# A graph network's edge stage: a third buffer of gathered rows, relu ahead of the query work, node sums added two batches behind

## The chip, the cores and the metric

One Trainium2 chip, one core. The metric is device time of one execution in microseconds, lower is better. Engines are named as in the profile: PE (TensorE), DVE (VectorE), ACT (ScalarE), POOL (GpSimd), SP (SyncE, which only issues DMAs here).

## What is computed

The layer has 6250 nodes of 256 channels and 106250 directed edges sorted by destination. Cut to the part that matters here:

```python
xn = layernorm(x)
msg = relu(xn[src] + edge_attr_256)          # 106250 x 256
agg = zeros.at[dst].add(msg)                 # node sums, 6250 x 256
h = (xn + agg) @ W1 + b1 ...                 # GNN network with batch, graph and node norms
# linear attention on xn: keys and queries centred, squared, divided by their sums
k2 = l2norm_over_nodes(k*k / (sum(k*k) + 1e-7));  q2 = l2norm_over_channels(q*q / (sum(q*q) + 1e-7))
attn = v + q2 @ (k2.T @ v) / sqrt(N);  mix = attn @ W_out + b_out
x = x + gnn + mix;  x = x + top2_of_8_experts(layernorm(x))
```

Everything is float32 in the edge stage.

## The kernel before

The program runs in stages with a barrier between them: `layernorm_stage` (normalised rows go to the DRAM table `xn_rows`, and transposed tiles stay in SBUF), `edge_mix_stage` (edges and attention, the stage of the change), `gnn_mlp_stage`, `residual_stage` and `moe_stage` (the experts).

**The edge stage** walks over NB = 104 batches of 1024 edges, 8 to a partition (EK = 8). For batch b:

- SP loads 1 MB of edge attributes into `EA[b % 3]` (L566), once the matmuls of batch b-3 are done.
- POOL gathers the source rows with eight indirect DMAs of 128 rows of 1 KB each (`gather`, L187) into `GA[b % 2]`. Before a batch with even b it waits until the rows of batch b-1 have landed (`RUN = 2`), and before each batch b >= 2 until DVE has added batch b-2.
- DVE (`add`) waits for attributes, gathered rows and `win_full` of batch b-2, and then runs eight pairs: a one-hot selection tile for the next batch (L611) and the sum of rows and attributes in place (L622).
- ACT (`relu`, L720) clears the negatives of the whole batch in one instruction.
- PE (`scatter`, L792) sums the messages into a window of 128 nodes in PSUM with eight float32 matmuls against the selection tiles, each of which the profile shows as two.
- DVE (`into_tiles`, L632) adds the window to `node_sum`, in two instructions. It does that for batch b-1 right behind `add(b)`.

**Beside the edges** the same loop carries the attention, one tile of 128 nodes per batch. In the first pass (batches 1 to 51) `keys`, `key`, `squared`, `scaled`, `fourth` and `key_sums` build the key statistics. At batch 52 `finish_keys` and `key_weights` close them. In the second pass (batches 54 to 103) `query_value` (L834 and L835), `query` (L743), `query_turns` (PE transposes, L841), `query_turned` (ACT copies them from PSUM, L757), `query_fourth` (L750), `query_norm` (L762), `mixed` (L850) and `residual` (DVE, L683 to L696, then a store by SP, L581) make the attention's output.

Order is written out by hand, one instruction stream per engine. In a batch of the second pass PE runs `query_value(t)`, `query_turns(t-1)`, `scatter(b)`, `mixed(t-1)`; ACT runs `query_fourth`, `query_turned`, then `relu(b)`, `query_norm`, `query`; DVE runs `add(b)`, `into_tiles(b-1)`, `residual(t-2)`. The window sums use two PSUM banks in turn.

## Time and profile before

| | us |
|---|---|
| median of 3 runs | 2473.62 |
| lowest, highest run | 2454.32, 2487.86 |
| span of the profiled execution | 2457.6 |
| edge stage: first gather of batch 0 to the last residual instruction | 71.0 to 1347.1 |
| gathers of batches 1 to 103 | 84.2 to 1322.3 |

The span runs from the first to the last instruction of the profiled execution. The three runs lie between 3.3 us below and 30.3 us above it, the median 16.0 us above. In the rows, a name such as `edge_attr` stands for all buffers of that name; "idle before" is how long the engine had done nothing before the instruction, and what ended that.

### The profile page before, as it was taken

How to read it: one execution, taken by the hardware profiler on the slowest of the kernel's cores; microseconds unless marked ns; L12 is line 12 of the kernel's file. 1: busy time of each engine (PE TensorE's matmuls, PEld its weight loads, DVE VectorE, ACT ScalarE, POOL GpSimd, SP SyncE). 2: the span in 40 equal slices, each digit the busy share in tenths (PEclk: the TensorE clock that was granted, in tenths of full speed). 3: DMA queues.
4: the chain of work that ended last, by engine and by line, in shares of the span. 5: the costliest groups of instructions: out<-in, count | busy, mean ns of one | idle time of the engine just before them, and what ended most of it. 6: DMA issues, size and time to landing. Idle time of an engine off the chain costs nothing. (4 is left out here: it accounts for less than half of the span.)

```text
span 2457.6 us, 34821 instructions
## 1 busy us (share of the span) xinstructions
PE 1823.5 (74%) x10022; PEld 1451.8 (59%) x10023; DVE 1286.6 (52%) x3862; ACT 823.3 (34%) x1606; POOL 1250.4 (51%) x1137
## 2 busy tenths in 40 slices
PE   3367665676667777777686889681279999999996
PEld 3245444455444555454454778571268888888885
DVE  7455455545555555554554444568954444444443
ACT  3122222222222222222222346557324444444442
POOL 1576676776776666666663000136424444444443
PEclk8587788777878877888788999755689999999998
DMA  6565565555655555655553100377213223223222
GB/s 234 175 210 186 183 200 181 195 188 184 203 182 183 189 187 191 197 184 178 183 189 123 23 1 0 94 213 222 77 25 50 43 45 48 45 44 49 45 43 35
DMA packets 129882, 320.95 MB, mean 131 GB/s; under 512 B 32234, under 2 KB 78729, under 8 KB 114427
## 3 DMA queue, kind: packets, MB, share of 16 engines
q0 software_dynamic: 66624, 157.12, 24.7%
q1 hardware_dynamic: 56908, 162.65, 19.1%
q10 hardware_dynamic: 6255, 0.10, 0.3%
q8 instruction: 36, 0.59, 0.1%
q14 instruction: 59, 0.48, 0.1%
HBM read 279.67 MB, written 40.12 MB: 130 GB/s over the span
## 5 line engine op out<-in xcount | busy, mean ns | idle before, releaser
L187 POOL DMA_INDIRECT gathered<-xn_rows,src_table x832 | 846.2, 1017 | 409.3 <-issue 253.8
L792 PE MATMUL bank<-edge_attr,dst_select 128*128 128x256 f32 x1664 | 562.9, 512 | 379.7 <-issue 194.7
L792 PEld LDWEIGHTS bank<-edge_attr,dst_select 128*128 128x128 f32 x1664 | 433.1, 267 | 506.8 <-issue 214.7
L611 DVE TENSOR_SCALAR dst_select<-iota_window,dst_partition 128x128 f32<-128x128 f32 x832 | 258.8, 312 | 379.5 <-DMA gathered<-xn_rows,src_table 315.5
L1751 PE MATMUL bank<-rowsT_parts,expert_weights 128*128 128x256 f16 x3564 | 409.5, 274 | 10.0 <-issue 6.3
L1751 PEld LDWEIGHTS bank<-rowsT_parts,expert_weights 128*128 x3564 | 346.7, 98 | 59.0 <-issue 17.9
L720 ACT ACTIVATE edge_attr<-edge_attr 128x2048 f32<-128x2048 f32 x104 | 198.3, 1906 | 514.0 <-DVE edge_attr L622 438.5
L622 DVE TENSOR_TENSOR edge_attr<-gathered,edge_attr 128x256 f32<-128x256 f32 x832 | 344.2, 414 | 0.0
L1712 POOL DMA_INDIRECT out<-expert_out,output_row_of_slot x108 | 184.2, 1705 | 300.4 <-ACTq L1810 278.0
L1857 DVE SCALAR_TENSOR_TENSOR gated<-bank,silu 128x512 f32<-128x512 f32 x216 | 120.7, 559 | 184.5 <-ACT silu L1796 172.8
L1764 PE MATMUL bank<-expert_weights,gated_parts 128*128 x1836 | 209.3, 273 | 0.4 <-DVE gated_parts L1865 0.4
L1764 PEld LDWEIGHTS bank<-expert_weights,gated_parts 128*128 128x128 f16 x1836 | 179.5, 98 | 21.5 <-issue 0.7
L1865 DVE TENSOR_TENSOR gated_parts<-gated,gated_parts 128x512 f16<-128x512 f32 x216 | 122.8, 568 | 124.9 <-ACT gated_parts L1800 124.1
L757 ACT ACTIVATE query_squaredT<-bank 128x256 f32<-128x256 f32 (+1 forms) x49 | 18.8, 383 | 452.1 <-PE bank L841 349.2
L1796 ACT ACTIVATE silu<-bank 128x512 f32<-128x512 f32 x216 | 104.6, 484 | 190.7 <-PE bank L1751 181.2
L1800 ACT ACTIVATE gated_parts<-gated 128x512 f16<-128x512 f32 x216 | 112.8, 522 | 150.0 <-DVE gated L1857 149.4
L632 DVE SCALAR_TENSOR_TENSOR node_sum<-bank,in_first_tile,node_sum 128x256 f32 x104 | 49.7, 478 | 212.7 <-PE bank L792 163.9
L67 POOL DMA_DIRECT2D out<-residual_in x20 | 14.1, 712 | 240.4 <-DVE residual_in L1369 239.9
L1702 POOL DMA_INDIRECT rows<-token_rows,row_of_slot x110 | 109.6, 997 | 50.0 <-issue 32.5
L1065 PE MATMUL bank<-activated,w_gnn 128*128 128x250 f32 x400 | 87.7, 383 | 9.0 <-ACT activated L1096 9.0
L834 PE MATMUL bank<-w_q_and_v_out,xnT 128*128 128x512 f32 (+1 forms) x196 | 92.1, 592 | 0.0
L1050 PE MATMUL bank<-node_sumT,w_gnn 128*128 128x256 f32 (+1 forms) x400 | 89.3, 377 | 0.0
(274 smaller groups left out, 2095.3 us busy)
## 6 DMA issues: line engine op xcount, KB each, us to landing
edge_attr<-in_edge_attr SPq DMA_DIRECT2D x104, 1024.0 KB
raw_weights<-in_L_ffn_w SPq DMA_DIRECT2D x16, 1088.0 KB, 5.1
gathered<-xn_rows,src_table POOLq DMA_INDIRECT x832
rows_in<-xn_rows SPq DMA_DIRECT2D x48, 128.0 KB
rows_in<-in_x SPq DMA_DIRECT2D x48, 128.0 KB
residual_rows<-residual_tile SPq DMA_DIRECT2D x48, 128.0 KB
residual_in<-residual_rows SPq DMA_DIRECT2D x10, 560.0 KB
out<-residual_in POOLq DMA_DIRECT2D x10, 560.0 KB, 4.4
```

Of the source, the lines that this page charges most:

```text
L187: pool.indirect_dma_start(out=k.GA[h][:, e, :], out_offset=None, in_=k.xn_d[:, :], in_offset=bass.IndirectOffsetOnAxis(ap=k.src[:, b, e:e ...
L611: dve.tensor_scalar(SEL[b % 3][:, e, :], k.iota[:, :], k.dstp[:, b, e:e + 1], None, ALU.is_equal)
L622: last = dve.tensor_tensor(ea[:, e, :], ga[:, e, :], ea[:, e, :], ALU.add)
L720: act.activation(EA[b % 3][:, :, :], EA[b % 3][:, :, :], ACT.Relu).then_inc(relu_done, 1)
L792: last = pe.matmul(WINP[b % 2][:, 0:C], SEL[b % 3][:, e, :], EA[b % 3][:, e, :], start=e == 0, stop=e == EK - 1)
L1702: pool.indirect_dma_start(out=XG[i % 2][:, t, :], out_offset=None, in_=k.tok_d[:, :], in_offset=bass.IndirectOffsetOnAxis(ap=k.row_of[:, a ...
L1712: pool.indirect_dma_start(out=k.acc_d[:, :], out_offset=bass.IndirectOffsetOnAxis(ap=k.sum_of[:, at:at + 1], axis=0), in_=YS[i % 2][:, t, ...
L1751: last = pe.matmul(bank[:, jj * TT:(jj + 1) * TT], w(e, wp, at + b * step, 128), X16[h][:, xp, b, :], start=n == 0, stop=n == 3 * CB - 1)
L1764: last = pe.matmul(YP[h][:, t * C:(t + 1) * C], G16[h][:, gp, j * TT + t * 128:j * TT + (t + 1) * 128], w(e, wp, W2S + j * C, C), start=n ...
L1800: last = act.activation(G16[h][at, 0, s * 512 + cols.start:s * 512 + cols.stop], GF[r][at, cols], ACT.Copy)
L1857: last = dve.scalar_tensor_tensor(GF[r][at, cols], (H1 if tail else H3)[r][at, cols], SG / (SX * SW), SIL[r][at, cols], ALU.mult, ALU.mult)
L1865: last = dve.tensor_tensor(low, GF[r][at, cols], G16[h][at, 0, to], ALU.subtract)
```

## The change

In the edge stage:

- A third buffer `gathered2` with its own semaphore (AHEAD = 3). POOL no longer waits for landed rows; before batch b it waits only until DVE has added batch b-3.
- `into_tiles` runs two batches behind `add` (LATER = 2), and `scatter(b)` gets a wait: `into_tiles(b-2)` must have emptied the PSUM bank that it writes. Until now that followed from DVE's order.
- ACT runs `relu(b)` ahead of `query_fourth` and `query_turned` of its batch.
- To make room, the query's squares and fourth powers use the key's buffers (`Q2, Q4 = K2[0:2], K2[2]`), the transposed squares use `K4`, and the residual tiles use `KB`. The first pass is done with them when the second begins.

```diff
--- before.py
+++ after.py
@@ -57,6 +57,7 @@
 
 
 
+AHEAD = 3
 SPLIT = TR // 16 * 16
 MOVED = 32
 
@@ -181,11 +182,11 @@
     return min(NP, N - t * NP)
 
 
-def gather(k, pool, b, h):
+def gather(k, pool, b, rows, done):
 
     for e in range(EK):
-        pool.indirect_dma_start(out=k.GA[h][:, e, :], out_offset=None, in_=k.xn_d[:, :],
-                                in_offset=bass.IndirectOffsetOnAxis(ap=k.src[:, b, e:e + 1], axis=0)).then_inc(k.g_in[h], 16)
+        pool.indirect_dma_start(out=rows[:, e, :], out_offset=None, in_=k.xn_d[:, :],
+                                in_offset=bass.IndirectOffsetOnAxis(ap=k.src[:, b, e:e + 1], axis=0)).then_inc(done, 16)
 
 
 def layernorm_stage(k, st):
@@ -328,7 +329,7 @@
                 store(n)
             pool.wait_ge(src_ready, 2)
             pool.wait_ge(xn_st, 16 * (NG + 1))
-            gather(k, pool, 0, 0)
+            gather(k, pool, 0, k.GA[0], k.g_in[0])
 
         @block.vector
         def _(dve):
@@ -500,8 +501,10 @@
 
     nc, sb, sem, A = k.nc, k.sb, k.sem, k.A
     two, three = range(2), range(3)
+    LATER = 2
     EA = [sb(f"edge_attr{h}", [128, EK, C], F32, st) for h in three]
-    GA, g_in = k.GA, k.g_in
+    GA = [*k.GA, sb("gathered2", [128, EK, C], F32, st)]
+    g_in = [*k.g_in, sem("gathered_in2")]
     SEL = [sb(f"dst_select{h}", [128, EK, NP], F32, st) for h in three]
     XT = [sb(f"rows_in{h}", [128, C], F32, st) for h in two]
     KB = [sb(f"key{h}", [128, C], F32, st) for h in two]
@@ -510,14 +513,13 @@
     KT = sb("key_sum_shifted", [128, 1], F32, st)
     VS = [sb(f"row_scaled{h}", [128, C + 1], F32, st) for h in two]
     K4 = [sb(f"key_fourth{h}", [128, C], F32, st) for h in two]
-    Q2 = [sb(f"query_squared{h}", [128, C], F32, st) for h in two]
-    Q4 = sb("query_fourth", [128, C], F32, st)
-    Q2T = [sb(f"query_squaredT{h}", [128, CB, NP], F32, st) for h in two]
+    Q2, Q4 = K2[0:2], K2[2]
+    Q2T = [K4[h][:, :].rearrange("p (b n) -> p b n", b=CB) for h in two]
     QS = sb("query_sums", [128, PT], F32, st)
     QF = sb("query_fourth_sums", [128, PT], F32, st)
     QN = sb("query_norms", [128, PT], F32, st)
     QD = [sb(f"query_scale{h}", [128, 1], F32, st) for h in two]
-    RT = [sb(f"residual_tile{h}", [128, C], F32, st) for h in two]
+    RT = KB
     KX = sb("key_by_node", [128, CB, C + 1], F32, st)
     KXT = sb("key_by_nodeT", [128, CB, C], F32, st)
     nrow = sb("key_norm_row", [1, C], F32, st)
@@ -539,7 +541,6 @@
         "query_value_full", "query_squared_done", "query_fourth_done", "query_norm_done", "queryT_full", "queryT_done",
         "mix_full", "residual_done"))
     stray_full, stray_out = sem("strays_summed"), sem("strays_copied")
-    RUN = 2
     P1, P2 = 1, PT + 5
     FIN = PT + 3
 
@@ -599,11 +600,9 @@
         @block.gpsimd
         def _(pool):
             for b in range(1, NB):
-                if b % RUN == 0:
-                    pool.wait_ge(g_in[(b - 1) % 2], 16 * EK * ((b - 1) // 2 + 1))
-                if b >= 2:
-                    pool.wait_ge(added, b - 1)
-                gather(k, pool, b, b % 2)
+                if b >= AHEAD:
+                    pool.wait_ge(added, b - AHEAD + 1)
+                gather(k, pool, b, GA[b % AHEAD], g_in[b % AHEAD])
 
         @block.vector
         def _(dve):
@@ -611,9 +610,9 @@
                 dve.tensor_scalar(SEL[b % 3][:, e, :], k.iota[:, :], k.dstp[:, b, e:e + 1], None, ALU.is_equal)
 
             def add(b):
-                ea, ga = EA[b % 3], GA[b % 2]
+                ea, ga = EA[b % 3], GA[b % AHEAD]
                 dve.wait_ge(ea_in[b % 3], 16 * (b // 3 + 1))
-                dve.wait_ge(g_in[b % 2], 16 * EK * (b // 2 + 1))
+                dve.wait_ge(g_in[b % AHEAD], 16 * EK * (b // AHEAD + 1))
                 if b > 1:
                     dve.wait_ge(win_full, b - 1)
                 for e in range(EK):
@@ -699,8 +698,8 @@
                 select(0, e)
             for b in range(NB):
                 add(b)
-                if b > 0:
-                    into_tiles(b - 1)
+                if b >= LATER:
+                    into_tiles(b - LATER)
                 if is_tile(b - P2 - 2):
                     residual(b - P2 - 2)
                 if is_tile(b - P1):
@@ -709,7 +708,8 @@
                     scaled(b - P1 - 1)
                 if b == FIN:
                     finish_keys()
-            into_tiles(NB - 1)
+            for b in range(NB - LATER, NB):
+                into_tiles(b)
             for t in range(NB - P2 - 2, PT):
                 residual(t)
 
@@ -762,11 +762,10 @@
                 act.activation(QN[0:v, t:t + 1], QF[0:v, t:t + 1], ACT.Sqrt).then_inc(qn_done, 1)
 
             for b in range(NB):
+                relu(b)
                 if is_tile(b - P2 - 1):
                     query_fourth(b - P2 - 1)
                     query_turned(b - P2 - 1)
-                relu(b)
-                if is_tile(b - P2 - 1):
                     query_norm(b - P2 - 1)
                 if is_tile(b - P2):
                     query(b - P2)
@@ -787,6 +786,8 @@
             pe.matmul(STRAY[0:1, 0:1], k.stray_col[:, :], k.ones[:, 0:1], start=True, stop=True).then_inc(stray_full, 1)
 
             def scatter(b):
+                if b >= LATER:
+                    pe.wait_ge(evac, b - LATER + 1)
                 pe.wait_ge(relu_done, b + 1)
                 for e in range(EK):
                     last = pe.matmul(WINP[b % 2][:, 0:C], SEL[b % 3][:, e, :], EA[b % 3][:, e, :], start=e == 0, stop=e == EK - 1)
```

## Rows read from the trace of the kernel before

**Rows 1.** The page, part 1: busy us, share of the span, instructions.
```profile
PE 1823.5 (74%) x10022; PEld 1451.8 (59%) x10023; DVE 1286.6 (52%) x3862; ACT 823.3 (34%) x1606; POOL 1250.4 (51%) x1137
```

**Rows 2.** Waits of POOL, 71 to 1340 us: engine, line, releaser, total us, times, longest.
```profile
POOL gathered L187 <- issue: 253.8, 772, 4.0
POOL gathered L187 <- DMA gathered<-xn_rows,src_table: 114.3, 49, 5.0
POOL gathered L187 <- DVE edge_attr L622: 33.6, 9, 6.1
```

**Rows 3.** Timeline of POOL, first pass, two batches: start us, duration us, instruction, idle before.
```profile
119.85 0.94 POOL L187 DMA_INDIRECT gathered<-xn_rows,src_table  x1 [2.02 <-DMA gathered<-xn_rows,src_table]
121.10 1.09 POOL L187 DMA_INDIRECT gathered<-xn_rows,src_table  x1 [0.30 <-issue]
122.50 1.29 POOL L187 DMA_INDIRECT gathered<-xn_rows,src_table  x1 [0.30 <-issue]
...
135.35 1.27 POOL L187 DMA_INDIRECT gathered<-xn_rows,src_table  x1 [0.30 <-issue]
136.94 1.29 POOL L187 DMA_INDIRECT gathered<-xn_rows,src_table  x1 [0.30 <-issue]
...
142.74 0.95 POOL L187 DMA_INDIRECT gathered<-xn_rows,src_table  x1 [2.01 <-DMA gathered<-xn_rows,src_table]
```

**Rows 4.** Timeline of DVE, first pass: the first of 16 instructions of an add, and what follows.
```profile
426.68 0.29 DVE L611 TENSOR_SCALAR dst_select<-iota_window,dst_partition 128x128 f32<-128x128 f32 x1 [6.56 <-DMA gathered<-xn_rows,src_table]
...
430.95 0.47 DVE L632 SCALAR_TENSOR_TENSOR node_sum<-bank,in_first_tile,node_sum 128x256 f32 x1
```

**Rows 5.** Busy time of every engine in the two passes.
```profile
core 0: us, PE busy (x) PEld busy (x) DVE busy (x) ACT busy (x) POOL busy (x), PEclk, DMA share, GB/s
84.00:720.00 636.00, 407.38 (x1368) 307.04 (x1369) 327.49 (x1191) 142.69 (x202) 445.06 (x435) 0.78 0.58 192
720.00:1323.00 603.00, 450.11 (x1336) 295.35 (x1335) 309.69 (x1106) 150.95 (x334) 393.42 (x390) 0.81 0.58 189
```

**Rows 6.** Waits of four engines in the second pass, 720 to 1323 us.
```profile
POOL gathered L187 <- DMA gathered<-xn_rows,src_table: 57.0, 22, 5.0
POOL gathered L187 <- DVE edge_attr L622: 33.2, 8, 6.1
...
PE bank L792 <- ACT edge_attr L720: 108.2, 29, 9.9
PE bank L792 <- issue: 44.7, 19, 3.7
...
ACT query_squaredT L757 <- remote: 102.8, 8, 14.7
...
DVE node_sum L632 <- PE bank L792: 147.9, 32, 12.9
```

**Rows 7.** Timeline of PE and ACT, one batch of the second pass.
```profile
869.48 1.03 PE L850 MATMUL bank<-kv_out_weights,query_squaredT 128*128 128x256 f32 x4
...
873.21 0.44 PE L841 MATMUL bank<-ident,query_squared 128*128 128x128 f32 x2
...
874.11 0.39 ACT L757 ACTIVATE query_squaredT<-bank 128x256 f32<-128x256 f32 x1 [9.93 <-PE bank L841]
874.39 1.90 ACT L720 ACTIVATE edge_attr<-edge_attr 128x2048 f32<-128x2048 f32 x1
...
876.34 6.68 PE L792 MATMUL bank<-edge_attr,dst_select 128*128 128x256 f32 x16 [2.70 <-ACT edge_attr L720]
...
882.86 1.03 PE L850 MATMUL bank<-kv_out_weights,query_squaredT 128*128 128x256 f32 x4
```

**Rows 8.** Timeline at the end of the stage.
```profile
1321.37 0.94 POOL L187 DMA_INDIRECT gathered<-xn_rows,src_table  x1 [0.30 <-issue]
...
1327.15 2.76 DVE L622 TENSOR_TENSOR edge_attr<-gathered,edge_attr 128x256 f32<-128x256 f32 x8
...
1346.71 0.42 DVE L696 TENSOR_TENSOR residual_tile<-residual_tile,bank 106x256 f32<-106x256 f32 x1
```

## The prediction

> **What bounds the kernel now.** I read the page first, then POOL's waits, then POOL's and DVE's timelines, and last the two passes apart. Part 1 of the page [rows 1] points at PE, busy for 74% of the span. That is an average over stages. In the edge stage the engine to look at is POOL, the one that gathers. Its waits [rows 2] are of three kinds: 253.8 us of "issue" in 772 pieces, which is 0.30 us between any two gathers with a few longer ones; 114.3 us in 49 waits for landed rows; 33.6 us in 9 waits for DVE's adds. The timeline [rows 3] shows the pattern of the first pass: 16 gathers in a row, 0.94 to 1.29 us each with 0.30 us between them, then one wait of 2.0 us until the last rows are in. A pair of batches takes 142.74 - 119.85 = 22.9 us. DVE starts its adds when the rows land, after 6.56 us of idleness, and needs 430.95 - 426.68 = 4.3 us for them [rows 4]. So in the first pass DVE, ACT and PE all hang on POOL, and POOL stops for nothing but the landing.
>
> The second pass is slower. From 84 to 720 us POOL issues 435 gathers, that is 54.4 batches at 11.7 us; from 720 to 1323 us it is 390 gathers, 48.75 batches at 12.4 us [rows 5]. POOL waits 57.0 us for rows and 33.2 us for adds there, DVE waits 147.9 us for the window sums, and PE waits 152.9 us for its messages [rows 6]. The timeline [rows 7] shows a circle: PE's transposes (873.21), ACT's copy of them (874.11), only then relu (874.39), then the scatter (876.34), which ends near 882.86 and lets DVE add the window, finish the residual and begin the next adds. Relu stands behind the copy on ACT, so 2.70 us of PE's time go by in each batch.
>
> **The change part by part.**
>
> *POOL's waits.* Both kinds are gone as long as DVE's add of batch b-3 is done when POOL begins batch b. Rows of batch b-1 land about 2 us into POOL's work on batch b, and their add takes 4.3 us; two batches earlier, the add of batch b-3 ended some 15 us before POOL wants its buffer for batch b. That is 114.3 + 33.6 = 147.9 us less [rows 2]. Each of the 58 waits leaves the ordinary 0.30 us of issue in its place, 17.4 us. Net: 130.5 us.
>
> *Gathers beside DVE.* A gather takes 0.95 us alone and up to 1.29 us beside the adds and selections. In a batch that began with a wait, POOL starts with DVE and two gathers are stretched, by 0.14 and 0.34 us (the rows at 121.10 and 122.50 in [rows 3]). In a batch without the wait they are stretched by 0.32 and 0.34 us (135.35 and 136.94 in [rows 3]). All batches will now be of the second kind: 0.2 us for each of 49, 10 us given back. Bounds: if no gather were stretched, the 824 gathers would shrink from 838.5/825 = 1.016 us [rows 5] to 0.95 us, 55 us less; if eight of eight took 1.29 us, the rival below. I take +10 us, as the unwaited batches show it.
>
> The Trainium skill speaks against this part. "SBUF — State Buffer", in "A bandwidth-pool intuition that's wrong (but worth ruling out)", says that GpSimd and a two-port DVE operation do not run together, "one fully blocks". By that rule each batch would cost eight gathers at 1.25 us plus the whole 4.3 us of adds, 14.3 us, and POOL could not go below that. The trace has batches of 10.5 us with the adds beside them, so the block holds here for part of the gathers only.
>
> *Landing of rows.* The rows must keep up with a POOL that never pauses. In the pair of [rows 3] the DMA engines followed 16 gathers and were 1.7 us behind the last (2.01 less 0.30). The longest such wait is 5.0 us [rows 2]. The DMA share is 0.58 [rows 5]; at 10.8 instead of 12.0 us a batch it becomes 0.65. I price this at nothing: a third buffer lets rows be late by most of a batch. If that cover is gone, it is the third rival.
>
> *Relu first.* ACT starts relu when the adds are done. In the second pass PE's 152.9 us of waiting [rows 6] lose their cause; PE then needs 603 - 152.9 = 450.1 us for 48.75 batches, 9.2 us each. Eight waits of ACT are marked "remote" and sum to 102.8 us, 12.9 us each against the usual 9.9 us [rows 6, 7]. I read the excess, 24 us, as something that held PE up unseen, 0.5 us a batch. So PE needs 9.7 us and POOL (603 - 90.2 + 9.0) / 48.75 + 0.1 = 10.8 us. POOL bounds this pass too, by 1.1 us. What moves behind relu (fourth powers, copy, norm) is needed by `mixed`, behind a scatter of 6.5 us; relu is 1.90 us and the copy 0.39 us [rows 7], so it is hidden.
>
> *Node sums two behind, and the new wait.* DVE no longer waits at `into_tiles`, since that window was summed a batch ago. But `residual` behind it still needs `mixed` of the batch before, which stands behind the same scatter, so in the second pass the 147.9 us of waiting mostly move to the residual's last instructions. That costs nothing while DVE has slack: it is busy 309.7 of 603 us [rows 5], 6.4 us a batch. The new wait of `scatter(b)` has `mixed` and all later PE work queued behind it, and DVE's next residual waits for those. It is met 1.0 us after the adds (two window adds of 0.47 us, the first in [rows 4]), while relu takes 1.90 us from the same point. It costs nothing; at worst, with DVE held in the residual of the batch before, the second rival.
>
> *Shared buffers.* The key tiles are last used at batch 51, the query tiles begin at 54. Nothing.
>
> *The end of the stage.* The last gather ends at 1322.3 us, the last residual at 1347.1 us [rows 8], 24.8 us later. In between the last adds begin only at 1327.15, because DVE was late with the residual. Without lag: 1.7 us landing, 2.8 us adds, 2.0 us relu, 6.5 us scatter and 1.0 us mixed [rows 7], and an estimated 2.5 us for the window's two adds and the five short instructions of the residual, 16.5 us. I take 8 us less; it could be 0, with PE still behind.
>
> *Sum.* -130.5 + 10 - 8 = -128.5 us. I add 6 us for moments in the second pass in which PE, 1.1 us a batch ahead on average, is late for longer than the buffers cover (bounds 0 and 81 us, the whole of POOL's gain there; nearest to zero, since 1.1 us a batch make up a loss quickly). That gives -122.5 us, a span of 2335.1 us. The page gives no time of the profiled execution itself; the median of the runs lies 16.0 us above its span, and with that I forecast 2351 us, 5% less. Runs of this kernel spread by 1.4%, so about 2% can be told from no change.
>
> **The rivals.**
>
> *PE becomes the bound of the second pass.* For it: PE is the busiest engine there, 450 of 603 us, and its scatter took 6.5 us of wall time in [rows 7] (876.34 to 882.86), its other work 4.2 us (869.48 to the end at 873.65), and the stalls add 0.5 us: 11.2 us a batch. With 0.3 us lost at each hand-over it is 11.5 us, 34 us more than POOL's 10.8 over the pass: 2379 us (2351 - 6 + 34). Against it: the granted clock averages 0.81 there [rows 5], and the scatters that took 6.5 us began after PE had stood idle; with less idleness it should not fall.
>
> *The rows, not POOL, set the pace (the change doesn't do what it says).* The software queue would be as fast as the pattern of 22.9 us a pair and no faster, DVE would wait as before, and only the end of the stage is saved: 2466 us. For it: waits of up to 5.0 us for landing [rows 2]. Against it: 16 gathers issued in 20.9 us were followed to within 1.7 us. "DMA: Bandwidth & Descriptors", in "Queues, rings and completion order" of the Trainium skill, says that each DMA engine takes turns between queues, a packet at a time, so a gather beside the 1 MB load of attributes gets only part of the engines. That would stretch the landing for the length of the load, not for good.
>
> *Slower.* POOL runs beside DVE's adds and beside unlanded rows all the time, and every gather takes the 1.29 us that is now the exception: 8 x (1.29 + 0.30) = 12.7 us a batch against 1238.1/103 = 12.0 us, 0.7 x 103 = 72 us more, less the end's 8 us: 2538 us. It decides from a mean gather of 1.20 us on. For it: 1.29 us is what a gather beside DVE costs. Against it: DVE's adds fill 4.3 of 10.8 us, and twelve of the sixteen gathers of [rows 3] did not exceed 0.95 us.
>
> **How the numbers follow.** Chances: forecast 0.70 (own range 2320 to 2375), PE bound 0.16 (2365 to 2400), rows set the pace wholly or in part 0.09 (2400 to 2470), slower 0.05. Predicted: 2351 us. Low end: shorter gathers could give up to 55 us, of which I allow 35: 2315 us. The high end takes in PE's case and the first part of the third: 2425 us. Faster by over 2% means below 2424 us: 0.70 + 0.16 + 0.02 = 0.88. Within 2%: 0.08. Slower: 0.04.
>
> **What would show it.** Right: POOL's waits for rows gone, gathers back to back at 0.30 us for whole passes, 10.7 to 10.9 us a batch in both, mean gather 1.02 to 1.05 us, last gather at about 1208 us, relu directly behind the adds in the second pass. PE's case: POOL waits for DVE's adds in the second pass, with PE's waits near nothing. The rows' case: DVE waits more than 6 us for rows and POOL for DVE. Slower: mean gather above 1.2 us. I am wrong at large if the stage still takes over 1200 us.

## The result, and the profile after

| | before, us | after, us |
|---|---|---|
| median of 5 runs each, in turn on one chip | 2477.99 | 2514.68 |
| lowest, highest run | 2454.32, 2487.86 | 2507.52, 2528.43 |
| span of the profiled execution | 2457.6 | 2526.8 |
| last gather issued, last residual instruction | 1322.3, 1347.1 | 1395.1, 1416.5 |

The ratio is 1.0165, with a 95% interval from 1.0115 to 1.0215: slower by 1 to 2%, where 5% faster was forecast. The whole loss lies in the edge stage, which ends 69.4 us later.

First POOL, since the forecast is a sum over POOL. These are its waits and the longest of ACT's and DVE's, from 71 to 1420 us (engine, line, releaser, total us, times, longest); they answer to [rows 2] and [rows 6]. Most lines of the changed kernel have moved by one: the gather is L188, relu L720, the adds L621, the scatter L793, `key` L639, the copies of the turned tiles L757 and the residual L693.

```profile
POOL gathered L188 <- issue: 248.8, 807, 2.1
ACT key_fourth L757 <- remote: 231.0, 13, 30.1
POOL gathered L188 <- DVE edge_attr L621: 225.8, 23, 15.0
...
ACT key_squared L727 <- DVE key L639: 202.0, 16, 23.8
DVE key L639 <- remote: 195.4, 14, 26.8
DVE key L693 <- remote: 182.1, 23, 16.7
...
PE bank L851 <- issue: 152.1, 9, 22.4
```

The waits for landed rows are gone, as the forecast said (114.3 us in [rows 2]). But 23 waits for DVE's adds stand there, 9.8 us each, where there were 9 of 3.7 us. POOL was to be free of those too. DVE in turn waits for something the profile calls "remote", up to 26.8 us at a time, and PE shows "issue" waits of up to 22.4 us. The two passes, with the columns of [rows 5]:

```profile
84.00:720.00 636.00, 382.24 (x1268) 267.00 (x1269) 301.56 (x1103) 139.56 (x196) 416.85 (x407) 0.73 0.54 179
720.00:1390.00 670.00, 412.58 (x1410) 266.20 (x1408) 322.31 (x1169) 152.82 (x327) 417.26 (x414) 0.80 0.56 180
```

In the same 636 us POOL issues 407 gathers where it issued 435, and every engine did less. No engine is the bound on average. So the place to look is what happens ahead of one of the 23 waits. This is the timeline of the changed kernel from 462 to 477 us, as PE, POOL, DVE and ACT lines stand in it (start, duration, instruction, idle before):

```profile
462.54 0.58 PE L793 MATMUL bank<-edge_attr,dst_select 128*128 128x256 f32 x1 [1.32 <-issue]
...
463.96 0.58 PE L793 MATMUL bank<-edge_attr,dst_select 128*128 128x256 f32 x1 [0.84 <-issue]
...
465.39 0.59 PE L793 MATMUL bank<-edge_attr,dst_select 128*128 128x256 f32 x1 [0.85 <-issue]
...
466.09 0.29 PEld L793 LDWEIGHTS bank<-edge_attr,dst_select 128*128 128x128 f32 x1 [1.11 <-issue]
466.79 0.59 PE L793 MATMUL bank<-edge_attr,dst_select 128*128 128x256 f32 x1 [0.81 <-issue]
...
472.14 0.94 POOL L188 DMA_INDIRECT gathered<-xn_rows,src_table  x1 [0.30 <-issue]
...
475.92 1.29 PE L799 MATMUL bank<-w_k,xnT 128*128 128x256 f32 x2 [0.81 <-issue]
...
476.71 0.42 DVE L639 TENSOR_TENSOR key<-bank,b_k_rows 128x256 f32<-128x256 f32 x1 [20.10 <-remote]
...
477.16 0.42 ACT L727 ACTIVATE key_squared<-key 128x256 f32<-128x256 f32 x1 [19.40 <-DVE key L639]
```

Look at PE's rhythm. The profile shows nothing that it waits for, yet it starts one matmul every 1.40 us, with the weight load half way between: 0.70 us for each instruction, whatever that is. A scatter of 32 instructions takes 22 us at this pace; it takes 3.6 to 6.8 us otherwise. I call such a standstill behind PE a crawl. DVE and ACT stand idle for 20 us, since all they have left depends on PE. POOL alone goes on, in steps of 1.25 us, until at 473.1 it has filled all three buffers and must stop. 2.8 us after its stop PE issues two matmuls back to back again, and POOL goes on at 482.4, when DVE has added. The stretches of this crawl one by one, with the columns of [rows 5]:

```profile
460.00:465.00 5.00, 2.38 (x5) 1.15 (x4) 0.00 (x0) 0.00 (x0) 3.78 (x5) 0.50 0.36 105
465.00:470.00 5.00, 2.16 (x4) 0.86 (x3) 0.00 (x0) 0.00 (x0) 3.78 (x5) 0.50 0.37 105
470.00:475.00 5.00, 1.83 (x4) 0.86 (x3) 0.00 (x0) 0.00 (x0) 2.48 (x3) 0.50 0.37 105
```

DMA share 0.37 at 105 GB/s: neither the engines of the DMA nor the memory are at a limit (0.54 over the pass). The granted clock is 0.50, its lower level of 1.2 GHz, but that makes a matmul 0.58 us long; it does not put 0.8 us of nothing behind it.

The rhythm is one of two faces. In the second pass most standstills look like this:

```profile
1012.46 0.44 PE L842 MATMUL bank<-ident,key_squared 128*128 128x128 f32 x2
1012.73 3.62 PE L793 MATMUL bank<-edge_attr,dst_select 128*128 128x256 f32 x16
...
1021.75 0.95 POOL L188 DMA_INDIRECT gathered<-xn_rows,src_table  x1 [0.30 <-issue]
1022.16 0.48 DVE L693 SCALAR_TENSOR_TENSOR key<-bank,query_scale,rows_in 128x256 f32<-128x256 f32 x1 [12.19 <-remote]
...
1023.00 0.95 POOL L188 DMA_INDIRECT gathered<-xn_rows,src_table  x1 [0.30 <-issue]
...
1041.08 0.38 ACT L757 ACTIVATE key_fourth<-bank 128x256 f32<-128x256 f32 x1 [30.09 <-remote]
```

By their rows PE's two transposes (L842) are done at 1012.9 and the scatter behind them at 1016.35, at full pace. ACT's copy of the transposes waits for their semaphore, and it starts at 1041.08, 28.2 us after they ended. The wait is called "remote" because no row of the program ends near the semaphore's update. So here PE's work, as recorded, is done and only its signal is late. (The ends of PE's rows are modelled, so they can be off by some part of a matmul; no model of a 0.3 us matmul makes 28 us.)

POOL pauses for over 1 us 25 times in the stage, and there are 31 stretches of over 7 us, 421 us together, in which neither DVE nor ACT does anything; before had none inside the stage. Ten of the 31 hold the rhythm of 0.70 us, nine of them in the first pass; most of the others end with a signal of PE that came over 5 us late. In 14 of them POOL's pause begins first and DVE or ACT come back 2.4 to 5.4 us later (158.1 and 163.5, 232.9 and 238.0, 346.6 and 350.8, and so on). In a fifteenth the pause begins 0.3 us before the end, and 16 end while POOL goes on issuing, as at 1022.16 above. So a stop of POOL may end a crawl, but a crawl also ends without one. Before, POOL stopped by itself every two batches.

### The profile page after: what moved, and what is told of

The parts are those of the page before. It is cut to its first block and busy times, and to the rows that moved or that the text cites. A ratio compares the mean times of both kernels' runs of the same rounds, so it can differ in the third digit from the quotient of the medians.

```text
span 2526.8 us, 34872 instructions
## 1 busy us (share of the span) xinstructions
PE 1767.0 (70%) x10022; PEld 1386.4 (55%) x10023; DVE 1280.8 (51%) x3862; ACT 825.7 (33%) x1606; POOL 1250.2 (49%) x1137
## 5 line engine op out<-in xcount | busy, mean ns | idle before, releaser
L188 POOL DMA_INDIRECT gathered<-xn_rows,src_table x832 | 845.9, 1017 | 482.3 <-issue 248.8
L793 PE MATMUL bank<-edge_attr,dst_select 128*128 128x256 f32 x1664 | 455.3, 426 | 215.1 <-issue 125.2
L793 PEld LDWEIGHTS bank<-edge_attr,dst_select 128*128 128x128 f32 x1664 | 347.4, 214 | 312.3 <-issue 225.2
L1752 PEld LDWEIGHTS bank<-rowsT_parts,expert_weights 128*128 x3564 | 346.1, 98 | 59.1 <-issue 18.2
L621 DVE TENSOR_TENSOR edge_attr<-gathered,edge_attr 128x256 f32<-128x256 f32 x832 | 344.4, 415 | 2.3 <-issue 2.3
L720 ACT ACTIVATE edge_attr<-edge_attr 128x2048 f32<-128x2048 f32 x104 | 198.6, 1910 | 384.9 <-DVE edge_attr L621 218.5
L851 PE MATMUL bank<-kv_out_weights,key_fourth 128*128 128x256 f32 (+1 forms) x196 | 63.4, 454 | 207.7 <-issue 152.1
L1765 PEld LDWEIGHTS bank<-expert_weights,gated_parts 128*128 128x128 f16 x1836 | 179.5, 98 | 21.5 <-issue 0.7
L851 PEld LDWEIGHTS bank<-kv_out_weights,key_fourth 128*128 128x128 f32 (+1 forms) x196 | 42.4, 224 | 220.4 <-issue 156.2
L639 DVE TENSOR_TENSOR key<-bank,b_k_rows 128x256 f32<-128x256 f32 (+1 forms) x49 | 20.4, 417 | 276.6 <-remote 195.4
L757 ACT ACTIVATE key_fourth<-bank 128x256 f32<-128x256 f32 (+1 forms) x49 | 18.6, 380 | 379.0 <-remote 231.0
L693 DVE SCALAR_TENSOR_TENSOR key<-bank,query_scale,rows_in 128x256 f32<-128x256 f32 (+1 forms) x49 | 23.7, 483 | 198.1 <-remote 182.1
```

Of the source, the lines that this page charges most:

```text
L188: pool.indirect_dma_start(out=rows[:, e, :], out_offset=None, in_=k.xn_d[:, :], in_offset=bass.IndirectOffsetOnAxis(ap=k.src[:, b, e:e + 1 ...
L621: last = dve.tensor_tensor(ea[:, e, :], ga[:, e, :], ea[:, e, :], ALU.add)
L720: act.activation(EA[b % 3][:, :, :], EA[b % 3][:, :, :], ACT.Relu).then_inc(relu_done, 1)
L793: last = pe.matmul(WINP[b % 2][:, 0:C], SEL[b % 3][:, e, :], EA[b % 3][:, e, :], start=e == 0, stop=e == EK - 1)
L1752: last = pe.matmul(bank[:, jj * TT:(jj + 1) * TT], w(e, wp, at + b * step, 128), X16[h][:, xp, b, :], start=n == 0, stop=n == 3 * CB - 1)
L1765: last = pe.matmul(YP[h][:, t * C:(t + 1) * C], G16[h][:, gp, j * TT + t * 128:j * TT + (t + 1) * 128], w(e, wp, W2S + j * C, C), start=n ...
```

## The experiments

The kernels ran in five sittings, each on one chip with its own runs of before; ratios are to those. The sittings differ in a way that turned out to matter, so each is given with what before took in it. "Idle stretches" are those of over 7 us with neither DVE nor ACT busy, inside the edge stage. Where POOL pauses on purpose, some of them are DVE's ordinary wait for rows and no crawl (5 in the first run below, the longest of 8.9 us).

### First sitting (before 2449.96 us): does the pause protect PE?

Theory A: POOL's unbroken stream of gathers makes PE crawl, and a pause ends or prevents it. Rivals: the new order (relu first, node sums two behind), or the third buffer itself.

The wait for landed rows put back into the changed kernel:

```diff
             for b in range(1, NB):
+                if b % 2 == 0:
+                    pool.wait_ge(g_in[(b - 1) % AHEAD], 16 * EK * ((b - 1) // AHEAD + 1))
                 if b >= AHEAD:
```

> The changed kernel with one thing undone: POOL again waits before every even batch until the rows of the batch before have landed. The third buffer, relu first, sums two behind and the shared homes stay. Theory A (an unbroken stream of gathers keeps PE from getting on; a pause of POOL ends it): PE's long crawls of 12 to 22 us are gone, POOL waits some 50 times about 2 us for rows and hardly for DVE, the stage has 10.8 to 11.7 us a batch, and the time is 2400 to 2470 us, below the kernel before. Theory B (the new order of ACT and DVE with PE's new wait makes the stalls): the crawls stay, and the time is 2500 us or more.

Measured: 2409.95 us, ratio 0.9826 (0.9796 to 0.9855), 105 us less than the changed kernel in its own sitting. POOL's waits:

```profile
POOL gathered L188 <- issue: 238.2, 779, 0.5
POOL gathered L188 <- DMA gathered<-xn_rows,src_table: 118.9, 51, 4.1
```

There is no wait for DVE left, although three buffers and the order are those of after. Adding waits of 118.9 us removed waits of 225.8 us.

The mirror image, before without its wait (two buffers, old order):

```diff
-                if b % RUN == 0:
-                    pool.wait_ge(g_in[(b - 1) % 2], 16 * EK * ((b - 1) // 2 + 1))
                 if b >= 2:
```

> The kernel before with one thing taken away: POOL's wait for landed rows before even batches. Two buffers, the old order of relu and sums and the old homes stay. Theory A: PE crawls appear here too, of 10 to 20 us about once in five batches, and the time is 2490 to 2600 us, slower than before. Theory B: no crawls, POOL's 114 us of waiting for rows turn into waiting for DVE's adds or into gain, and the time is 2380 to 2480 us.

Measured: 2537.0 us, ratio 1.0367 (1.0304 to 1.043), 14 idle stretches of 176 us, 228.5 us in 39 waits of POOL for DVE. This and the kernel before, in one sitting, differ in nothing but that wait: taking it out is enough to lose more than the whole change loses.

The third buffer with the order of before:

```diff
-    LATER = 2
+    LATER = 1
...
-                relu(b)
                 if is_tile(b - P2 - 1):
...
                     query_turned(b - P2 - 1)
+                relu(b)
+                if is_tile(b - P2 - 1):
...
-                if b >= LATER:
-                    pe.wait_ge(evac, b - LATER + 1)
```

> The changed kernel with the old order: relu behind the query work, sums one batch behind, no new wait of PE. The third buffer, no wait for landed rows and the shared homes stay. Theory A: crawls as in the changed kernel, since POOL is as free as there; 2500 to 2560 us. Theory B: crawls gone, the first pass at 10.7 us a batch, 2370 to 2430 us.

Measured: 2548.55 us, ratio 1.0387 (1.0344 to 1.0431), 16 idle stretches of 228 us. POOL's waits:

```profile
POOL gathered L188 <- issue: 251.6, 791, 2.1
...
POOL gathered L188 <- DVE edge_attr L621: 230.6, 38, 19.2
```

So the new order is not what slows the change. It may soften it: the changed kernel had 1.0165 and, below, 1.0196, in other sittings.

A pause that waits for nothing: eight small memsets, each with a drain, ahead of every even batch, in the changed kernel. Whatever has landed or not, POOL issues no gather for a while.

```diff
             for b in range(1, NB):
+                if b % 2 == 0:
+                    for _ in range(PAUSES):
+                        pool.memset(pause[:, :], 0.0)
+                        pool.drain()
```

> The changed kernel, where POOL before every even batch does eight small memsets with a drain behind each, some 2 to 4 us, and waits for no rows. Theory A, in the form that any pause in the issue of gathers is enough: crawls gone or cut to the few us until the next pause, 2400 to 2480 us. If instead it is the wait for landing that matters and not the pause: crawls stay, 2500 us or more plus some of the memsets' time. Theory B: 2500 us or more.

Measured: 2591.53 us, ratio 1.0562 (1.0529 to 1.0595). The crawls are gone, as theory A has it, and the time is far above its range, since the pause came out at 6.1 us from one gather to the next and not at 2 to 4. No wait is called "remote" (the first run has 11 such waits, 32.8 us), POOL never waits for DVE or for rows, and a pair of batches takes 26.9 us, the pause and 16 gathers of 1.01 us with 0.30 us between them. POOL's groups (busy, mean ns, idle before):

```profile
L189 POOL DMA_INDIRECT gathered<-xn_rows,src_table x832 | 840.4, 1010 | 283.6 <-issue 276.0 <-DMA xn_rows<-node_sum 4.3 <-POOLq L240 3.4
...
L607 POOL MEMSET pause_tile<- 128x128 f32 x408 | 97.7, 239 | 176.5 <-issue 142.2
```

A wait for a semaphore of the rows is not needed, then, to keep PE going. The run can't tell a pause in issuing from the landing of the rows, though: waits for rows last 2.3 us on average in the run with the landed wait (118.9 us in 51), so in 6.1 us the rows have landed too. To tell the two apart takes a shorter pause in a sitting with crawls, and no run has that.

### Second sitting (before 2430.37 us): more instructions for PE, other pauses

In the first pass of after the idle stretches begin 212 or 318 rows of PE apart (weight loads and matmuls), but for two that are 53 apart. The profile shows 16 KB packets of instructions in a DMA queue of their own:

```profile
q8 instruction: 37, 0.61, 0.1%
```

The 22 of them from 143.8 to 1405.8 us stand 255 instructions of PE apart on average ((5840 - 477) / 21, by the count of PE's records). The Trainium skill, "Runtime: NRT & Kernel Launch", "Instruction fetch mechanics", says that an engine's program arrives in blocks of 16 KiB, 256 instructions, and that the crossing is "mostly hidden". The size agrees with these packets. Once a block is about as often as the crawls come. The loads themselves are not slow, 0.9 to 1.5 us each, and they don't stand where the crawls do: 6 of the 31 idle stretches have one in them, 0.7 to 2.2 us after their start, and none ends with one. That a crawl follows from such a block is the idea that I tested: with more instructions in the program there should be more crawls. Forty waits that are always met went ahead of each scatter:

```diff
                 pe.wait_ge(relu_done, b + 1)
+                for _ in range(40):
+                    pe.wait_ge(stray_full, 1)
```

> The changed kernel with 40 more PE instructions a batch, each a wait for a semaphore that came long ago, ahead of the scatter. Theory A1 (what the stream of gathers holds up is the loading of PE's instructions, which comes once per block of its program, so that a crawl belongs to every so many instructions): the crawls come about twice as often in batches, every two to three batches instead of every five; the time rises by 150 us or more, to over 2650 us. Theory A2 (the gathers hold up PE's work itself, whatever its instructions): crawls as often as in the changed kernel; some 2 us of waits a batch lie mostly beside other work, 2500 to 2600 us.

Measured: 2319.86 us, ratio 0.9546 (0.9527 to 0.9565). No crawl at all, no idle stretch, no pause of POOL, where both theories had over 2500 us. It runs as the forecast had it. Its POOL waits and passes:

```profile
POOL gathered L188 <- issue: 252.9, 830, 0.3
```

```profile
84.00:720.00 636.00, 445.32 (x1496) 332.51 (x1497) 354.34 (x1288) 156.78 (x233) 491.96 (x473) 0.81 0.64 210
720.00:1180.00 460.00, 382.03 (x1207) 251.05 (x1206) 276.09 (x989) 130.99 (x301) 355.18 (x345) 0.86 0.69 222
```

473 gathers in 636 us are 59.1 batches at 10.76 us, and 345 in 460 us are 10.67 us a batch. A DMA share of 0.64 to 0.69 goes with no crawl here, where the crawls had 0.37: a busy set of DMA engines is not by itself what PE suffers from.

This looked as if more instructions cured PE. That was wrong, as the fourth sitting showed, and in this sitting nothing else was run that could have told it: the changed kernel itself was missing. The other three kernels were variants of the pause.

The landed wait of the first sitting ahead of every fourth batch:

```diff
+                if b % 4 == 0:
+                    pool.wait_ge(g_in[(b - 1) % AHEAD], 16 * EK * ((b - 1) // AHEAD + 1))
```

> As e1, but POOL waits for landed rows only before every fourth batch. Theory A: a pause every 46 us or so leaves room for crawls of up to two or three batches' gathers, so they come back in part: between e1 and the changed kernel, 2420 to 2500 us. If a pause every four batches is as good as one every two, the waits saved (25 times 1.7 us) show as gain: 2370 us on the scale of e1's 2410.

Measured: 2366.08 us, 0.9732 (0.9715 to 0.9748).

Ahead of every batch:

```diff
+                pool.wait_ge(g_in[(b - 1) % AHEAD], 16 * EK * ((b - 1) // AHEAD + 1))
```

> As e1, but POOL waits for landed rows before every batch. Theory A: the rest of the PE stalls (46 us in six stretches over 7 us in which DVE and ACT both do nothing, in e1) goes, but 51 more waits of 1.7 us cost 87 us of POOL's time: 2440 to 2500 us. If stalls still cost e1 much more than seen, it is below 2410 us.

Measured: 2476.54 us, 1.0193 (1.0176 to 1.021); 102 waits of 2.08 us, 211.8 us.

Three small memsets ahead of every even batch, a pause of 1.3 us on average from one gather to the next, with no regard to landing:

```diff
+                if b % 2 == 0:
+                    for i in range(PAUSES):
+                        pool.memset(pause[:, :], 0.0).then_inc(paused, 1)
+                        pool.wait_ge(paused, (b // 2 - 1) * PAUSES + i + 1)
```

> The changed kernel, where POOL before every even batch does three small memsets, each waited for by POOL itself, about 1 us, and waits for no rows. It is shorter than the 1.7 us that the last rows need to land. If any gap in the issue of gathers lets PE on: crawls gone and about 30 us less than e1, near 2380 us. If the rows in flight must have landed first: crawls stay, 2500 us or more.

Measured: 2369.99 us, 0.9752 (0.9735 to 0.9768).

None of the four crawled. So they price pauses, and say nothing on what cures PE.

### Third sitting (before 2429.96 us): what of PE's extra work matters?

Two more wide matmuls a batch instead of the waits (their result is overwritten by the scatter's first matmul):

```diff
+                for _ in range(2):
+                    pe.matmul(WINP[b % 2][:, 0:2 * C], SEL[b % 3][:, 0, :], EA[b % 3][:, 0:2, :].rearrange("p e c -> p (e c)"), start=True, stop=True)
```

> The changed kernel with two more matmuls of 512 columns a batch ahead of the scatter (their sums are overwritten by it): about 2 us more of PE's time a batch, as the 40 waits of e5 take, with 8 instead of 40 more instructions. If e5 lost its crawls because PE comes later (its pace): crawls gone here too, 2320 to 2350 us. If it is the number or the kind of instructions: crawls stay, 2500 us or more.

Measured: 2318.68 us, 0.954 (0.9524 to 0.9556).

Twelve waits instead of forty:

```diff
+                for _ in range(12):
+                    pe.wait_ge(stray_full, 1)
```

> As e5 with 12 instead of 40 waits a batch, some 0.6 us. If the waits help in proportion: crawls fewer and shorter, between e5's 2320 us and the changed kernel's 2510. If a few instructions are enough to change how PE's program is loaded: no crawls, 2310 us.

Measured: 2320.65 us, 0.9555 (0.9537 to 0.9573). That two so different additions, and a third of one, all gave 2319 to 2321 us was the first sign that the additions had no part in it.

Before without its wait, with the forty waits of PE:

```diff
-                if b % RUN == 0:
-                    pool.wait_ge(g_in[(b - 1) % 2], 16 * EK * ((b - 1) // 2 + 1))
...
+                for _ in range(40):
+                    pe.wait_ge(stray_full, 1)
```

> e2 (the kernel before without POOL's wait for landed rows) with the 40 PE waits of e5 a batch. If the crawls are all that stood against taking the wait away, it loses them too and is faster than the kernel before; with two buffers and the old order PE's circle in the second pass stays, some 2 us longer by the waits: 2370 to 2430 us. If the waits help only with the new order: crawls, 2500 us or more.

Measured: 2356.68 us, 0.9702 (0.9684 to 0.972), where the same kernel without PE's waits had 1.0367 in the first sitting. POOL still waits 25.2 us for DVE, in 17 waits, which the three buffers with the new order don't have in this sitting.

The third buffer with the order of before (the diff of the first sitting) and with the landed wait:

```diff
+                if b % 2 == 0:
+                    pool.wait_ge(g_in[(b - 1) % AHEAD], 16 * EK * ((b - 1) // AHEAD + 1))
```

> e1 with the old order: the third buffer and POOL's wait for landed rows before even batches, relu behind the query work, sums one batch behind, no new wait of PE. It splits the gain of e1 (2410 against 2450 us) between the buffer and the order. By PE's circle of the second pass (relu behind the copy) the order has most of it: 2440 to 2455 us here on a scale where before has 2450. If the buffer has it: 2410 us.

Measured: 2413.18 us, 0.9926 (0.9907 to 0.9945). The time is that of the second case and the ratio lies between the two, since before itself took 20 us less in this sitting; the split that I wanted can't be read from it.

### Fourth sitting (before 2453.23 us): the same kernels again

The changed kernel unaltered, and three kernels from above with nothing changed. If the additions cure PE, they do so here too. If it was the sitting, they crawl here.

> The changed kernel itself, unaltered, beside e5, e9 and e2 on one chip and in one sitting. In the sitting of e1 to e4 the kernel before took 2450 us, in the next two 2430 us, so e5, e9, e10 and e11 may have met a quieter chip rather than cured anything. If the extra PE instructions or work cure the crawls: this has crawls and takes 1.01 times the kernel before or more, while e14 and e15 take 0.955. If the sitting is what differs: this too takes 0.95 times the kernel before, about 2310 us against 2430, with no crawl and no pause of POOL.

Measured: 2501.63 us, 1.0196 (1.0157 to 1.0234), 22 pauses of POOL, 29 idle stretches of 368 us.

> e5 again (40 more PE instructions a batch). Cure: 0.955 of the kernel before whatever e13 does. Sitting: it goes as e13 goes, within 1%.

Measured: 2528.15 us, 1.0272 (1.0211 to 1.0332). The same kernel took 2319.86 us in the second sitting. Its waits and passes now:

```profile
POOL gathered L188 <- issue: 250.5, 804, 3.0
POOL gathered L188 <- DVE edge_attr L621: 230.3, 26, 15.0
```

```profile
84.00:720.00 636.00, 389.11 (x1282) 267.42 (x1281) 303.89 (x1112) 141.43 (x196) 418.93 (x409) 0.74 0.55 180
720.00:1180.00 460.00, 294.64 (x943) 183.94 (x942) 218.57 (x791) 104.03 (x219) 283.04 (x282) 0.79 0.55 177
```

One stretch of PE's timeline, first as it ran in the second sitting:

```profile
458.25 5.38 PE L795 MATMUL bank<-edge_attr,dst_select 128*128 128x256 f32 x16 [3.17 <-issue]
463.47 1.03 PE L801 MATMUL bank<-w_k,xnT 128*128 128x256 f32 x4
```

and as it ran in the fourth:

```profile
456.52 3.04 PE L795 MATMUL bank<-edge_attr,dst_select 128*128 128x256 f32 x6 [4.03 <-issue]
460.38 0.58 PE L795 MATMUL bank<-edge_attr,dst_select 128*128 128x256 f32 x1 [0.82 <-issue]
462.50 0.58 PE L795 MATMUL bank<-edge_attr,dst_select 128*128 128x256 f32 x1 [1.53 <-issue]
...
475.80 0.58 PE L795 MATMUL bank<-edge_attr,dst_select 128*128 128x256 f32 x1 [0.81 <-issue]
```

Sixteen matmuls in 5.4 us there, and here ten of them still to come after the first six, one every 1.4 or 2.1 us. One program, two behaviours. POOL paused 28 times here against 22 in the unaltered kernel beside it, and 30 blocks of instructions were loaded against 23. More blocks go with more pauses, which fits the idea of the blocks and does not prove it: after itself had 25 pauses with 22 blocks.

> e9 again (two more wide matmuls a batch). Cure: 0.955 of the kernel before whatever e13 does. Sitting: it goes as e13 goes, within 1%.

Measured: 2515.36 us, 1.026 (1.0219 to 1.0301), 31 idle stretches of 399 us; 0.954 in the third sitting.

> e2 again (the kernel before without POOL's wait for landed rows), which took 1.037 of the kernel before with crawls. Cure by extra PE work: crawls here again, 1.03. Sitting: 0.965 to 0.975, as e11 had with its extra waits (0.970).

Measured: 2552.35 us, 1.0377 (1.0324 to 1.043), as in the first sitting.

So the additions cure nothing. What differs is the sitting. It is not the chip alone: the first sitting, with crawls, and the third, without, were on the same one. Before shows the difference too, faintly: it took 2450 to 2478 us, and its runs spread over 16 to 34 us, where the kernels without pauses crawl; it took 2430 us with a spread of 3 to 7 us where none did.

The traces tell the two kinds of sitting apart without any time. Page part 6 gives for each DMA the median time to landing, if all updates of its semaphore were recorded. Of the attributes' load it says in after:

```profile
edge_attr<-in_edge_attr SPq DMA_DIRECT2D x104, 1024.0 KB
```

and in the kernel with forty waits as it ran in the second sitting:

```profile
edge_attr<-in_edge_attr SPq DMA_DIRECT2D x104, 1024.0 KB, 5.3
```

In the first the landing is missing, because updates are. Counted in the trace files over the whole execution, and beside it the copies of turned tiles (49 in a run) for which ACT stood idle and which it began over 1.5 us after the end of PE's transposes:

| run | sitting | updates recorded | late copies | latest, us |
|---|---|---|---|---|
| before | of the result | 13,627 | 8 | 7.7 |
| after | of the result | 11,374 | 16 | 28.2 |
| landed wait put back | first | 11,741 | 10 | 8.3 |
| before without its wait | first | 12,922 | 12 | 21.8 |
| long pause (ACT waited for one copy only) | first | 13,118 | 0 | |
| after again | fourth | 11,447 | 21 | 21.5 |
| before without its wait, forty waits | third | 25,776 | 0 | |
| twelve waits | third | 25,782 | 0 | |
| landed wait, old order | third | 25,784 | 0 | |

All traces of the second, third and fifth sittings have 25,776 to 25,934 updates and no late copy; those of the other sittings have 11,374 to 13,627, whatever the kernel, and what is missing belongs to the edge stage: in after 475 of the 1114 updates of PE's, DVE's and ACT's instructions there have none recorded near their end, and 2 in all other stages. The zeros of the two kernels in the old order are the telling ones: ACT waited for all 49 copies, and each began 0.04 us after the transposes. So in the sittings with crawls the recording itself loses updates while POOL gathers. That opens a rival that no run tests: PE may be held up by the recording of its own work and signals, and not by the gathers as such. Every run on record has a span and a granted clock of its own, so none is known to have run without such recording. A time of before and after taken with no recording at all would decide it.

### Fifth sitting (before 2428.09 us): the short pauses again

What was left to ask is whether the cheaper pauses protect PE where it crawls. The two variants were run again in the hope of such a sitting, with nothing changed.

> The kernel after with POOL's wait for landed rows ahead of every fourth batch. Theory A (an unbroken stream of gathers slows PE's instruction stream, and any pause of POOL ends it; a pause need not come every two batches): where the kernel before takes 2450 us or more, this kernel shows no stretch over 7 us with neither DVE nor ACT busy and takes 0.965 to 0.985 of before. Theory B (the pause must come every two batches, since a slowed stretch runs until the next pause): it shows such stretches of some 5 to 15 us and takes 0.985 to 1.01. Where the kernel before takes 2430 us, both say 0.97, as measured there once.

Measured: 2366.32 us, 0.9742 (0.9726 to 0.9758).

> The kernel after with three small memsets (about 1.2 us of POOL) ahead of every even batch, and no wait for landed rows. Theory A (a pause in issuing is enough, whether or not the rows have landed): where the kernel before takes 2450 us or more, no stretch over 7 us with neither DVE nor ACT busy, and 0.97 to 0.99 of before. Theory B (the DMA queues must run empty, as they do in a wait for landed rows): the slowed stretches stay, and it takes 1.01 to 1.03. Where the kernel before takes 2430 us, both say 0.975, as measured there once.

Measured: 2365.55 us, 0.974 (0.9724 to 0.9756).

By before's 2428 us this was another sitting without crawls. The numbers of the second sitting are confirmed and the question stays open.

### One sum for all versions

POOL's gathers with the idle time before them (and the memsets with theirs) add up to the stage. Against the kernel with twelve waits (861.7 + 260.4 = 1122.1 us of POOL, 2320.65 us):

| version | POOL total, us | more than 1122.1 | 2320.65 plus that | measured |
|---|---|---|---|---|
| wait every four batches | 859.4 + 312.1 | 49.4 | 2370.1 | 2366.08 |
| short pause | 861.8 + 275.4 + 38.2 | 53.3 | 2374.0 | 2369.99 |
| wait every two | 851.8 + 364.8 | 94.5 | 2415.2 | 2409.95 |
| wait every batch | 838.3 + 443.1 | 159.3 | 2480.0 | 2476.54 |
| long pause | 840.4 + 283.6 + 274.2 | 276.1 | 2596.8 | 2591.53 |
| after, profiled execution | 845.9 + 482.3 | 206.1 | 2526.8 | 2528.43 |

All agree within 6 us. This is bookkeeping and no test of a cause: POOL is either issuing or idle from the first gather to the last, so the table shows that nothing behind the gathers changed by more than 6 us. Each version's time is set by what POOL does between them. What the forecast left out is the 225.8 us that POOL waits for DVE in after.

## Why the prediction was wrong

**What bounds the kernel, and the floor: right.** This is read from the three kernels that ran without a pause, and they are after with work added to PE. POOL's steps of 10.7 to 10.8 us a batch were forecast as 10.7 to 10.9, and the mean gather of 1036 ns as 1.02 to 1.05 us. They took 0.954 to 0.9555 of before; 2351 us of 2473.62 is 0.950. The terms of the sum, from the trace of before to that of the kernel with forty waits:

- *Gathers beside DVE*, +10 us: 862.2 - 846.2 = 16.0 us. The step was right, its size a little low.
- *The end of the stage*, -8 us: in the kernel with forty waits the last gather ends at 1189.5 us and the last residual at 1207.9, 18.4 us in place of 24.8, so -6.4 us.

```profile
1188.53 0.95 POOL L188 DMA_INDIRECT gathered<-xn_rows,src_table  x1 [0.30 <-issue]
```

```profile
1207.48 0.42 DVE L695 TENSOR_TENSOR key<-key,bank 106x256 f32<-106x256 f32 x1
```

- *POOL's waits*, -130.5 us: it was 147.9 + 253.8 - 252.9 = 148.8 us. The longer ones among the pieces of "issue", up to 4.0 us in [rows 2], went too, and I had left them in.
- +6 us for moments in which PE is late: none was seen.

Together -139.2 us, and 1347.1 - 139.2 is 1207.9, where the stage ends. In part that is the sitting and not the change: before took 2430.37 us beside that kernel, which is 110.5 us more than its 2319.86, against the 122.5 us of the forecast. So the likeness of the two sums is partly luck: the forecast starts from a before that had late signals in it, and the kernel with forty waits had none.

**"Both kinds are gone as long as DVE's add of batch b-3 is done": the step that failed.** I took it as met, with "some 15 us" in hand, and priced the waits for DVE's adds at nothing. A crawl eats these 15 us, since DVE's add stands in DVE's stream behind work that waits for PE: the line at 476.71 above waited 20.10 us, and POOL's next gather came only behind the adds that followed it:

```profile
482.37 0.94 POOL L188 DMA_INDIRECT gathered<-xn_rows,src_table  x1 [9.29 <-DVE edge_attr L621]
```

In after the condition fails 23 times, and the 225.8 us that POOL then waits are more than the 206.1 us of POOL's time that separate 2528 from 2320 us.

**Why I didn't see it: "something that held PE up unseen, 0.5 us a batch".** Eight waits of ACT in [rows 6] are marked "remote" and last 12.9 us where 9.9 is the usual. I read them as a constant of the kernel and carried them over into the new sum as 24 us. They are PE's signals come late. This is the latest of them:

```profile
1113.14 0.44 PE L841 MATMUL bank<-ident,query_squared 128*128 128x128 f32 x2
...
1121.27 0.38 ACT L757 ACTIVATE query_squaredT<-bank 128x256 f32<-128x256 f32 x1 [14.47 <-remote]
```

The eight copies began 1.9 to 7.7 us after the transposes had ended, 35.7 us together, and 36 of the other 41 within 0.05 us. In the same kernel without its wait and with forty waits of PE, in the third sitting, all 49 were on time. So the eight were no constant of the kernel. In after such a signal came up to 28.2 us late. I asked what each wait cost and not what it might keep from happening. That POOL's wait matters where PE crawls is shown by two kernels of one sitting that differ in it alone, 1 and 1.037; beside them the third buffer took 0.983 with the wait and 1.039 without it in the old order, and a long pause in its place left no crawl. That POOL's pauses ended before's eight is not shown: in six of them one had begun 1.1 to 4.2 us before the copy, in two it began after.

**The rivals.** Nothing came of the case that the rows set the pace: POOL waited for DVE, never for rows, and in the kernels without crawls rows kept up with a POOL that never paused. PE did not become the bound of the second pass: 10.67 us a batch there at a clock of 0.86. The slower case came true in sign, with another mechanism; its own condition, a mean gather of 1.20 us, was far off (1.017 us). That the result was slower is no merit of its chance. A batch of 14.3 us was worked out from the rule of the Trainium skill's "SBUF — State Buffer", in "A bandwidth-pool intuition that's wrong (but worth ruling out)", that "one fully blocks"; 10.7 us were measured. That speaks against my working, which let the block last for the whole 4.3 us of adds, and not against the rule: a gather was stretched by 0.34 us at most in [rows 3], no more than one of DVE's instructions takes (312 ns for a selection tile and 414 ns for an add, on average in before).

**Relu first, sums two behind: a gain is likely, its size is not shown.** No two runs of one sitting differ in the order alone. With the landed wait the old order took 0.9926 (2413.18 us) and the new 0.9826 (2409.95 us) in another sitting, in which before took 20 us more; by the times there is no difference, by the ratios 1%. Where PE crawls, the old order took 1.0387 and the new 1.0165 to 1.0196. In the third sitting two buffers in the old order took 2356.68 us and three in the new order 2318.68 to 2320.65 us: 36 to 38 us, 1.5%, for the third buffer and the order together.

**What stays open.** Why PE's instructions or their signals come late in some sittings while POOL issues without a break, and not in others. The loading of PE's program, in blocks of 256 instructions, fits how often it happens. It does not fit the standstill at 1012 to 1041 us, where PE's instructions were there, and done by their rows, and a signal was still missing; nor do most loads stand in a crawl. The recording, which loses updates in just these sittings, is the other suspect, and no run separates the two, or either from other paths that signals may share with POOL's descriptors. Nor is it known what makes a sitting one or the other. The unaltered after was never run in a quiet sitting; that it would take 2320 us is inferred from three kernels that only add work to it.

## What to carry to other kernels

A wait is not only a cost: before removing one, ask what it keeps apart, and read every stall that the profile can't explain ("remote", "issue" of several us) as a thing with a beginning and an end, not as a constant. When several engines idle together, look at the spacing of single instructions on the one that still moves, and at the time from the end of an instruction to the start of the one that waits for it. See whether the trace is whole: a landing time that is missing on the page was the sign here. And an experiment that "cures" something must run beside the uncured kernel in the same sitting; more instructions for PE looked like a cure here (0.955) and were none (1.027).

Of the versions run, the one with three buffers, the new order and the landed wait every two batches is the one to keep: 0.983 (0.9796 to 0.9855) where PE crawls without it. With a wait every four batches or a pause of about 1 us it is 0.974 in quiet sittings, and with no pause 0.955, but a kernel with no pause loses 2 to 4% in the others, and for the short pauses that was not tried.

## What the runs showed of the hardware

- In some sittings, with POOL issuing indirect DMAs every 1.25 us without a break, PE's instructions slow to 0.70 us each, LDWEIGHTS and MATMUL alike, for 6 to 17 us at a time in after, at a DMA share of 0.37, or PE's signals come up to 28.2 us after the recorded end of its work. Of 31 such stretches in after 14 ended 2.4 to 5.4 us after POOL had paused, and 16 while it went on. A wait of POOL of some 2 us every two batches went with signals at most 7.7 and 8.3 us late, and a pause of 6.1 us with no "remote" wait at all.
- It happens in some sittings and not in others: the same kernel took 2319.86 and 2528.15 us, 9% apart, while before moved by 1%. The traces of those sittings lack half of the semaphore updates (11,374 to 13,627 recorded, against 25,776 to 25,934), so that the recording may have a part in it.
- In the other sittings POOL's stream of 832 gathers ran at 1036 ns + 0.30 us each for the whole stage, beside DVE's adds and a DMA share of 0.69, with no sign of a limit of the queue.
